# The last attention head and the start of the output stage: other kinds of score units, the list scatter's owner freed, and a new order of loads

## The reference

```python
xn = _layernorm(x)                                   # x: 2 x 2048 x 512, 16 heads of 32
q, k, v = (proj(Wq, bq), proj(Wk, bk), proj(Wv, bv))
scores = q k^T / sqrt(32) + slope[h] * distance      # causal
ctx = softmax(scores) v
attn = ctx @ Wo + bo
topw, topi = top_k(softmax(rmsnorm(xn) @ router_w.T), 2)
y = sum over the two experts: share * (silu(xn @ gate_w[e]) * (xn @ up_w[e])) @ down_w[e]
out = x + attn + y * 4
```

## Time and profile before

| | us |
|---|---|
| median of three runs (1922.46 to 1927.61) | 1926.85 |
| the profiled execution, its own time | 1924.57 |
| its span in the profile | 1922.8 |
| PE busy in the span | 1870.5 (97%) |
| DVE, ACT, POOL busy | 1506.5, 1415.9, 1406.0 |

### The profile page before, as it was taken

One profiled execution on the slowest core, in us unless ns is written; L12 is line 12 of the kernel. 1 busy time (PEld: TensorE's weight loads), 2 busy tenths in 40 slices (PEclk: granted clock), 3 DMA queues, 4 the chain that ended last, 5 costly groups with the idle time before them and its releaser, 6 DMA issues. The chain is left out here.

```text
span 1922.8 us, 39426 instructions
## 1 busy us (share of the span) xinstructions
PE 1870.5 (97%) x8656; PEld 1441.3 (75%) x8657; DVE 1506.5 (78%) x3497; ACT 1415.9 (74%) x2790; POOL 1406.0 (73%) x1214
## 2 busy tenths in 40 slices
PE   6999999999999999999999999999998989999997
PEld 5788777777777777777777777777756767888875
DVE  6454466898999989999999998999957956666664
ACT  4333322999999999999999999999972235555554
POOL 5111113899999999999999999999948846666665
PEclk9999999999999999999999999999999999999998
DMA  8577767542423424234242342423217756556553
GB/s 274 199 245 257 270 221 235 143 106 63 107 74 77 106 63 110 71 78 104 63 111 70 79 103 63 119 63 83 77 41 230 251 178 122 103 104 108 104 98 65
DMA packets 119242, 242.14 MB, mean 126 GB/s; under 512 B 17632, under 2 KB 54368, under 8 KB 112896
## 3 DMA queue, kind: packets, MB, share of 16 engines
q1 hardware_dynamic: 101120, 205.84, 36.7%
q0 software_dynamic: 18080, 35.81, 10.2%
HBM read 139.28 MB, written 104.21 MB: 127 GB/s over the span
## 5 line engine op out<-in xcount | busy, mean ns | idle before, releaser
L1175 POOL TENSOR_TENSOR probs_lo<-probs,probs_hi 128x512 fp32r<-128x512 f32 x812 | 1020.2, 1300 | 79.4 <-ACT probs L1210 76.4
L1209 ACT ACTIVATE probs_hi<-s_ps 128x512 fp32r<-128x512 f32 x967 | 680.9, 704 | 26.1 <-DVE s_ps L1282 22.2
L1210 ACT ACTIVATE probs<-s_ps 128x512 f32<-128x512 f32 x933 | 637.5, 702 | 10.2 <-DVE s_ps L1282 6.6
L1261 DVE TENSOR_REDUCE m_part<-m_ps 128x1 f32<-128x512 f32 x744 | 477.8, 682 | 3.0
L1518 PE MATMUL s_ps<-q_st,k_st 100*128 100x512 f32 (+3 forms) x880 | 310.5, 385 | 1.1 <-DMA q_st<-m_rows 0.8
L1502 PE MATMUL m_ps<-k_st,q_st 98*128 98x512 f32 (+2 forms) x840 | 291.1, 382 | 1.3 <-DVE v_raw L776 0.8
L1537 PE MATMUL o_ps<-probs_hi,v_split 128*96 128x512 f32 (+3 forms) x741 | 272.4, 375 | 1.7 <-POOL probs_lo L1175 1.7
L1538 PE MATMUL o_ps<-probs_lo,v_split 128*96 128x512 f32 (+3 forms) x741 | 273.8, 371 | 0.0
L1258 DVE CUSTOM_DVE_ANT_0 m_ps<-m_ps,mask_row 128x128 f32<-128x128 f32 x496 | 244.4, 493 | 16.4 <-PE m_ps L1502 7.8
L1518 PEld LDWEIGHTS s_ps<-q_st,k_st 100*128 100x128 f32 x880 | 162.9, 190 | 61.3 <-ACT probs L1210 22.0
L623 POOL TENSOR_TENSOR v_rows<-v_raw,v_rows 128x512 fp32r<-128x512 f32 x32 | 41.3, 1294 | 228.9 <-ACT v_rows L679 228.9
(11 more groups left out here) (236 smaller groups left out, 3728.3 us busy)
## 6 DMA issues: line engine op xcount, KB each, us to landing
v_d<-v_rows SPq DMA_DIRECT2D x7, 3072.0 KB, 9.4
v_split<-v_d SPq DMA_DIRECT2D x22, 768.0 KB, 8.3
k_st<-k_hi_d SPq DMA_DIRECT2D x44, 256.0 KB
q_st<-q_hi_d SPq DMA_DIRECT2D x44, 256.0 KB
xn_d<-xs SPq DMA_DIRECT2D x8, 1024.0 KB, 11.8
q_hi_d<-qk_hi SPq DMA_DIRECT2D x32, 256.0 KB, 7.7
q_lo_d<-qk_lo SPq DMA_DIRECT2D x32, 256.0 KB, 7.8
k_hi_d<-qk_hi SPq DMA_DIRECT2D x32, 256.0 KB, 3.5
```

The lines of the kernel that those rows point to most:

```text
L1175: nc.gpsimd.tensor_tensor(*low_operands(u), ALU.subtract).then_inc(lo_ready_pool, 1)
L1209: nc.scalar.activation(probs_hi[:, P_SLOT[u]], scores, ACT.Exp, scale=SCALE)
L1210: nc.scalar.activation(scores if kind == "Q" else probs[:, P_SLOT[u]], scores, ACT.Exp, scale=SCALE).then_inc(p_ready, 1)
L1261: V.tensor_reduce(top, scores, AX.X, ALU.max).then_inc(m_taken, 1)
```

## The change

In the last head, units 15 to 33 but for 17, 20, 23, 26, 29 and 32 become Q, and all others W, so no P is left and POOL has no `probs_lo` of its own there. `place_tokens` begins at u1 and takes two or three steps a unit. `count_tokens` moves from u9 to u6, `share_weights` from u6 to u1, `high_wo` from u11, u13, u15, u17 to u3 to u6, `spread_matrix` from u5 to u1, and `first_inverses` on DVE from u4 to u16. The split of Wo moves from POOL (u24) to DVE (u22). On SP the inverses' store and load, and the load of `sums_first`, now stand behind the second O of the last head itself, and a load of the second output unit's sums, `sums_second`, is added behind them. In the output stage SP issues the bias row first, then x, then the sums of units 2 and 3; `last_inverses` moves behind unit 3, with its store and load at units 3 and 4; DVE makes the low part of unit 1 before the bias of unit 0; and ACT waits for that low part before it splits the second half of the weights, since `sums_second` lies where that half goes.

```diff
-LAST_WHOLE = [u for u in range(NS) if u not in (21, 23, 25, 27, 29, 30)]
+LAST_WHOLE = (*range(15), 17, 20, 23, 26, 29, 32)
-LAST_KIND = "".join("PW"[u in LAST_WHOLE] for u in range(NS))
+LAST_KIND = "".join("QW"[u in LAST_WHOLE] for u in range(NS))
...
+        if 0 < u <= NS and LAST_KIND[u - 1] == "Q":
+            order.append(("D", u - 1, 0))
...
+                sums_second = at("sums_second", k_slot[0] + 4 * S, [P, G, UW], F32)
...
-                    if (kind, u, back) == ("O", QCS - 1, 1):
+                    if (kind, u, back) == (("O", QCS - 1, 1) if maxima else ("O", 1, 0)):
...
+                sp.wait_ge(tokens_placed, 1)
+                sp.dma_start(sums_second, t["ctx_d"][0:D, UW:2 * UW].rearrange("(g p) n -> p g n", p=P)).then_inc(sums_loaded[1], 16)
...
-                    if is_last(n) and (kind, u) == ("S", 24):
-                        split_wo()
...
-                    if is_last(n) and kind == "S" and 10 <= u < 10 + 2 * G and u % 2:
-                        high_wo((u - 10) // 2)
+                    if is_last(n) and kind == "S" and 3 <= u < 3 + G:
+                        high_wo(u - 3)
...
-                        for _ in range((u >= 3) + (u >= 8) + (u >= 13)):
+                        for _ in range((u > 0) + (u > 0 and u != 4) + (u > 0 and not s_diagonals(u) and u != 4)):
...
-                        if u == 4:
+                        if u == 16:
                             first_inverses()
-                        if u == 5:
+                        if u == 22:
+                            dve.wait_ge(wo_hi_ready, G)
+                            V.tensor_tensor(t["wo_lo"], t["wo_raw"], t["wo_hi"].bitcast(F32), ALU.subtract).then_inc(wo_lo_ready, 1)
+                        if u == 1:
                             spread_matrix()
...
-                    if not maxima and (kind, u) == ("S", 9):
+                    if not maxima and (kind, u) == ("S", 6):
                         count_tokens()
...
-            load_sums(1)
+            sp.dma_start(bo_row[:, :], t["bo"].partition_broadcast(P)).then_inc(bo_loaded, 16)
             load_x(0)
-            sp.dma_start(bo_row[:, :], t["bo"].partition_broadcast(P)).then_inc(bo_loaded, 16)
+            load_sums(2)
+            sp.wait_ge(sums_loaded[1], 16)
+            load_sums(3)
...
-                if u < NU - 2:
+                if 2 <= u < NU - 2:
...
+                if u == 1:
+                    act.wait_ge(lo_ready, 2)
                 nc.scalar.activation(half(w_hi, u), half(w_raw, u), ACT.Copy).then_inc(w_hi_ready, 1)
...
+                if u == 0:
+                    context_low(1)
                 if u == 0:
                     dve.wait_ge(bo_loaded, 16)
                 add_bias(u)
-                if u + 1 < NU:
+                if 0 < u < NU - 1:
                     context_low(u + 1)
                 take(u)
-                if u == 0:
+                if u == 3:
                     last_inverses()
```

More of the change, by code:

```diff
@@ L1006, in attend @@
     tokens_placed = t["tokens_placed"]
-    sums_first, hi_first, lo_first, sums_loaded = (t[name] for name in ("sums_first", "hi_first", "lo_first", "sums_loaded"))
+    sums_first, sums_second, hi_first, lo_first, sums_loaded = (
+        t[name] for name in ("sums_first", "sums_second", "hi_first", "lo_first", "sums_loaded"))
     k_ones, q_ones, st_loaded, v_loaded, m_placed = t["k_ones"], t["q_ones"], t["st_loaded"], t["v_loaded"], t["m_placed"]
@@ L1180, in step_n @@
                         low_part(n - back, u)
-                    if is_last(n) and (kind, u) == ("S", 24):
-                        split_wo()
-            def split_wo():
-                pool.wait_ge(wo_hi_ready, G)
-                nc.gpsimd.tensor_tensor(t["wo_lo"], t["wo_raw"], t["wo_hi"].bitcast(F32), ALU.subtract).then_inc(wo_lo_ready, 1)
             step_n(0, before=False)
@@ L1232, in step_n @@
                         take_sums(n - back, u)
-                    if is_last(n) and kind == "S" and u == 6:
+                    if is_last(n) and kind == "S" and u == 1:
                         share_weights()
@@ L1604, in output @@
         t[name] for name in ("wo_hi_ready", "wo_lo_ready", "ctx_ready", "hi_ready", "lo_ready"))
-    hi_first, lo_first, sums_loaded = (t[name] for name in ("hi_first", "lo_first", "sums_loaded"))
+    sums_second, hi_first, lo_first, sums_loaded = (t[name] for name in ("sums_second", "hi_first", "lo_first", "sums_loaded"))
     KH = KD // 2
@@ L1637, in output, with sums_of @@
         block = t["block"]
+        def sums_of(u):
+            return sums_second if u == 1 else sums[:, u % 2]
         def half(w, u):
@@ L1693, in _ @@
                 sp.dma_start(x_rows(t["out"], u), xb[:, u % X_RING]).then_inc(stored[u % X_RING], 16)
-                if u == 0:
+                if u == 3:
                     store_inverses()
-                if u == 1:
+                if u == 4:
                     load_inverses()
@@ L1737, in _ @@
                     act.wait_ge(projected, u + 1)
-                    nc.scalar.activation(ctx_hi[:, u % 2], sums[:, u % 2], ACT.Copy).then_inc(hi_ready, 1)
+                    nc.scalar.activation(ctx_hi[:, u % 2], sums_of(u), ACT.Copy).then_inc(hi_ready, 1)
+                if u == 1:
+                    act.wait_ge(lo_ready, 2)
                 nc.scalar.activation(half(w_hi, u), half(w_raw, u), ACT.Copy).then_inc(w_hi_ready, 1)
@@ L1748, in context @@
                 dve.wait_ge(inv_spread, u // 2 + 1)
-                V.tensor_tensor(sums[:, u % 2], sums[:, u % 2], inv_ps[:, :, u % 2 * UW:(u % 2 + 1) * UW],
+                V.tensor_tensor(sums_of(u), sums_of(u), inv_ps[:, :, u % 2 * UW:(u % 2 + 1) * UW],
                                 ALU.mult).then_inc(ctx_ready, 1)
@@ L1753, in context_low @@
                 dve.wait_ge(hi_ready, u + 1)
-                V.tensor_tensor(ctx_lo[:, u % 2], sums[:, u % 2], ctx_hi[:, u % 2].bitcast(F32), ALU.subtract).then_inc(lo_ready, 1)
+                V.tensor_tensor(ctx_lo[:, u % 2], sums_of(u), ctx_hi[:, u % 2].bitcast(F32), ALU.subtract).then_inc(lo_ready, 1)
             def weights_low(u):
```

## The result

The changed kernel takes **1975.64 us** (median of four, 1972.83 to 1980.29) beside 1925.66 for the kernel before: a ratio of 1.0263, 95% interval 1.0249 to 1.0278. Forecast were 1912 and a range of 1906 to 1920. The profiled execution took 1977.54 us, its span is 1975.6. A few executions of the kernel before, and of some experiments, were some 48 us longer as well (1971 to 1980, 5 of 31 in one series of the kernel before), and the ratios leave them out.

The account below looks back on a forecast made before the run. PE was taken as busy except for waits and low clock in the last head, output stage and step to the experts; 0.5 - 6.8 - 6.9 = -13.2 from 1924.57 gave 1911.4, stated as 1912, range 1906 to 1920.

Parts of the forecast that it names:

- the step to the experts: Between output stage and experts: scatter ends by 1525, rows come early, PE's 5.86 us wait goes; -6.9 us.
- slower: Rival, chance 0.04: the wait at u18 drops the clock to 1.2 GHz, lasting through output units 0 and 1; 1937 us.
- The last head: Units 15 to 33: less PE work and old losses gone, against new waits and a low-clock stretch; +0.5 us in all.
- Wait (1): Last head, u18's score: PE waits 2.4 us for the bank of u15, which DVE's low part frees.
- wait (2): Last head, u24's score: PE waits 1.3 us because DVE's split of Wo stands ahead of u21's low part.
- the small waits: Last head, QQW triples: ACT and PE tie, so masks, third block's sums and `sums_first`'s high part show, about 3.0 us.
- The low clock that should have followed: Last head: one stretch of three microseconds at half speed after a long wait, in two of three cases; 1.0 us.
- the 4.5 "lost" before: Last head of the kernel before: 27.0 us against 22.5 of PE work; the 4.5 us lost were to go.
- The output stage: Sums of unit 1 ready beforehand and bias row first, so most of the 7.7 us lost there goes; -6.8 us.
- The wait at unit 2: Output stage: PE waits 0 to 1.9 us for unit 2's high part, taken as 0.5.
- the prediction's own term for `last_inverses`: Output stage: the inverses behind unit 3 stand ahead of unit 5's sums and cost PE 0.4 us more.
- all three signs: Signs of being wrong: a PE wait for `xg`, over 2 us at unit 2 or 5, output stage starting past 1450.

Follow-up runs that it names:

- paced_two: The changed kernel with two small GpSimd memsets behind each scatter, which then come 1.54 us apart: 1917.14 us, ratio 0.9964 to the kernel before.
- output_alone: The kernel before with only the change's edits of the output stage and the load of `sums_second`, its last head as before: 1927.04 us, ratio 1.0002.
- lists_held: The changed kernel with one more wait, so that the scatter begins only when the last head's sums are added: 1932.03 us, ratio 1.0027 to before.

## Why the prediction was wrong

**The failed step** is in "the step to the experts": "At 1.67 the 64 end by 1418 + 107 = 1525". It took the pace of a scatter that DVE holds up in the output stage for one that begins beside another mix of work, and it costed the moved scatter at nothing for the other engines. The four scatters at 1.30 stood in the same rows; they were its true pace, and the scatter ran at it. What the runs showed in its place: begun early and at 1.27 us, the scatter makes PE's unit 1 take 50 us instead of 5.7, with PE's signals to ACT and DVE up to 52.1 us late, and the kernel 58.5 us longer than with the scatters 1.54 us apart. By what path it does so stays open. No rival had a scatter that harms anyone but DVE. The rival "slower" had the low clock as its cause; the clock was indeed 0.50 from 1468 to 1516, but with PE busy for 3.5 to 4.1 us of each 16 there, and matmuls of 0.59 us are a small part of 2.80.

What the terms were worth without the stretch shows in `paced_two`. Timeline of PE, the waits in the last head, the spreads, the step (for the earlier trace rows):

```profile
1425.31 0.55 PE L1521 MATMUL s_ps<-q_st,k_st 100*128 100x128 f32 x2 [2.53 <-DVE probs_lo L1269]
...
1432.14 0.49 PE L1521 MATMUL s_ps<-q_st,k_st 100*128 100x512 f32 x1 [1.03 <-DVE probs_lo L1269]
...
1446.89 1.17 PE L1828 MATMUL inv_ps<-inv_st,spread_r 32*128 32x512 f32 x4
...
1461.73 2.13 PE L1848 MATMUL out_ps<-wo_hi,ctx_hi 128*128 128x512 f32 x8 [0.95 <-ACT ctx_hi L1750]
...
1467.54 1.19 PE L1828 MATMUL inv_ps<-inv_st,spread_r 32*128 32x512 f32 x4
...
1481.51 1.40 PE L1828 MATMUL inv_ps<-inv_st,spread_r 32*128 32x512 f32 x4 [1.35 <-issue]
1482.83 3.45 PE L1848 MATMUL out_ps<-wo_hi,ctx_hi 128*128 128x512 f32 x8
...
1549.48 2.04 PE L1848 MATMUL out_ps<-wo_hi,ctx_lo 128*128 128x512 f32 x8
1551.73 1.06 PE L2108 MATMUL xt_ps<-consts,xg 128*128 128x128 f32 x8 [0.22 <-DVEq L2087]
1553.86 0.49 PE L2117 MATMUL h_ps<-gu_hi,ex_hi 128*128 x1 [1.07 <-DVE ex_lo L2065]
```

- **The last head**: from the first score (1400.65) to the first spread 46.2 us, 44.5 before: +1.7 for a forecast +0.5. Wait (1) was 2.53 for 2.4, wait (2) 1.03 for 1.3, the small waits with that of the first value product (0.87, not foreseen) 3.0 for 3.0. The low clock that should have followed did not come (1.00 from 1418 to 1478); in the changed kernel it did, 0.50 at 1429 behind 2.51 us of waiting. That leaves 2.4 us which stand in no wait. Some 1.3 of them are the 4.5 "lost" before, which were too many: 1.66 of wait and some 1.5 at the low clock can be seen. The other 1.1 is open.
- **The output stage**: to its last matmul's start 102.6 us, 106.3 before: -3.7 for -6.8. The wait at unit 2 is 0.95, within its 0 to 1.9. What was missed are the next two pairs, 13.97 and 14.07 us for 12.56. The 1.35 at 1481.51, put down to issue, is a wait for DVE: in the code this spread needs the sums of unit 5, and they end at 1481.45, behind the inverses (timeline of DVE):

```profile
1476.58 1.74 DVE L1789 RECIPROCAL inv<-inv 128x256 f32<-128x256 f32 x1
...
1480.24 1.21 DVE L1763 TENSOR_TENSOR sums<-sums,inv_ps 128x1024 f32<-128x1024 f32 x1
```

So it is the prediction's own term for `last_inverses`, 1.35 for 0.4: the forecast let unit 5 wait for these sums, but the spread ahead of it waits for them already. Behind it come eight matmuls of 3.45 us, at the low clock.
- **The step to the experts**: from that start to the first expert matmul 4.4 us, 10.5 before: -6.1 for -6.9. The rows came in time though the scatter ended at 1533.3, not 1525.
- **The sum** is 1.7 - 3.7 - 6.1 = -8.1 for -13.2; the median fell by 6.9 (1924.02 to 1917.14). So even without the stretch the forecast of 1912 was 5 us too low, but on the right side. The stretch costs 1975.64 - 1917.14 = 58.5 (the two medians are from different series).

By the letter all three signs by which the prediction said it would be seen to be wrong were there: a wait of over 2 us at unit 2 (3.96), as the tail of a stretch that it had no sign for; a PE wait for `xg`, 1.56 us at the second tile (1616.86), where the kernel before has none, and 1.50 in `paced_two` too; and a stage that starts past 1450 (1451.08), which is the 3.9 us of the first 370. None of them points at what happened.

## What to carry to other kernels

A run of GpSimd indirect DMAs is not free for the rest of the core because its engine is idle: look at its spacing in the trace, and ask what held it to that spacing before you move it to a place where nothing does. Where idle time is put down to issue or to a remote signal, look up in the code what the instruction waits for and when that ended: here most of it on ACT and DVE was PE's signal, up to 52 us late, and some on PE itself was DVE. Two memsets between such DMAs (1.54 us apart instead of 1.27) won back 58 us here and left the kernel 0.36% below the one before.

## What was not expected of the hardware

- 64 scatters of 128 entries each, 1.27 us apart, made PE's matmuls come singly and its signals reach ACT and DVE up to 52.1 us late, until some 6 us behind their end, with the DMA engines at a share of 0.03; 1.54 us apart they did so in none of ten executions. DVE and ACT answered each other within 0.1 us meanwhile.
- The stretch is also met by chance: the kernel before, whose scatters come 1.65 us apart in the mean, had 5 executions of 31 at 1971 to 1980. They were not profiled, so that theirs is the same stretch is inferred from the time and from `output_alone` and `lists_held`.
- Single matmuls came at multiples of 0.70 us (2.10, 2.80), and SP took 0.69 us for an issue that took 0.34 without a stretch; why is open.
